# The second batch's x by rows, turned on TensorE, and a new order of the opening, in a transformer block on one core

## The chip, the core and the metric

The kernel runs on one core of one Trainium2 chip. The metric is the device time of one execution in microseconds (us); lower is better. A core has TensorE (PE in the profile, its weight loads PEld), VectorE (DVE), ScalarE (ACT), GpSimd (POOL) and SyncE (SP), which issues most of the DMAs. Each engine works through its own queue in order; they meet at semaphores.

## What is computed

Eight sequences (B = 8) of 1024 tokens of 128 numbers pass through single-head causal attention with a partial rotary embedding, a layer norm, a feed-forward layer with binarized weights and a second layer norm, all in float32:

```python
q, k, v = x @ wq, x @ wk, x @ wv                      # (8, 1024, 128) each
q, k = fractional_rope(q) / sqrt(128), fractional_rope(k) / sqrt(128)
s = q @ k.T - 1e30 * (i < j)
x = layernorm(x + softmax(s) @ v @ wo)
bw1, bw2 = mean(|w|, axis=1) * sign(w) for w1, w2     # (512, 128), (128, 512)
x = layernorm(x + gelu(x @ bw1.T + b1) @ bw2.T + b2)
```

## The kernel before

A batch c (0 to 7) is one sequence. Its 1024 tokens are 8 tiles (rows r, 0 to 7) of 128, in two halves h of 4 tiles, so that a half fills one PSUM bank of 512 columns. PSUM is held as two single banks (`next_bank`) and three pairs (`next_pair`), each handed out in turn: a task waits (`wait_freed`) until the task that had the same bank or pair three pairs or two banks earlier has been read out.

For a batch, the steps are these. x, transposed to `xT`, is split into a rounded part `xT_hi` (ScalarE, `xT_high`) and the rest `xT_lo` (GpSimd, `xT_low`; for batch 0 VectorE, `x0T_low`). `project(h, c)` makes q and k of a half with 12 matmuls of 256 columns into a pair (L631 to L633). VectorE multiplies by the tables (`rotate`, L1565 to L1568), ScalarE copies the pair to `tok` (`tok_copy`), GpSimd adds the rotated parts (`rotation_sum`, L340), TensorE turns q and k (`turn_qk(n, c)`, L641; n = 0, 1 are q and k of the first half, 2, 3 of the second), ScalarE and VectorE split them (`qkT_high`, `qkT_low`). `scores(r, c)` fills a pair; VectorE takes the maximum of the row (`row_max`, L1417), ScalarE the exponential (`exponentials`, L964). The turned probabilities come in one of two ways: in most rows VectorE transposes squares of 32 x 32 (`turn_row`, L1427) and 16 DMAs a group put the squares in place (`carry(g, c)`, L238); in rows 4 to 7 of the first and the last batch TensorE turns them (`turn_row` on TensorE, L658) and ScalarE and VectorE copy them (`row_copy`). `weigh_group` and `weigh_row` multiply with x itself (row tiles `xa[c % 2]`), `project_out` with the product of wv and wo. Then come the first norm, the feed-forward layer and the second norm.

For batch 0, x is loaded as rows into `xa[0]` and turned by TensorE (`turn_x0`). For the batches from 1 on, `xT` comes in a second load: four DMAs a batch (`stripes(c)`) bring stripes of 32 columns of x into `xq`, with pieces of 128 bytes, and VectorE transposes each half in squares (`x_squares`, L1544). The rows of x are loaded too (`tokens(c)`), since the weighing and the residual need them.

The order of each engine's queue is written out by hand, as a flat list of calls, and all lists overlap the batches: the opening below has work of batches 0, 1 and 2 side by side. The one-off preparation of the weights stands among them: `setup_wqk`, `setup_turn_wv`, `setup_wvT` and `setup_wvo` for attention, and for the feed-forward layer `setup_signs` (VectorE, four instructions on 512 columns in SBUF, L1394 to L1398), the turns `setup_turn_sgn1` and `setup_turn_sgn2` (TensorE, L532 and L540), `setup_magnitudes` and `setup_weights` (VectorE). In VectorE's queue of before the stretch from the first row_max reads: row_max(0, 0), row_max(1, 0), x_squares(0, 2), row_max(2, 0), x_squares(1, 2), turn_row(0, 0), row_max(3, 0), setup_wvo, turn_row(1, 0), (2, 0), (3, 0), qkT_low(3, 0), rotate(0, 1), rotate(1, 1), row_max(4, 0), setup_signs, row_max(5, 0), (6, 0), (7, 0), setup_magnitudes.

## Time and profile before

| | us |
|---|---|
| median of three runs | 292.16 (291.0 to 292.31) |
| the profiled execution, its own time | 291.92 |
| its span in the trace | 290.1 |
| TensorE busy | 264.5 (91%) |
| VectorE busy | 230.4 (79%) |
| ScalarE busy | 228.1 (79%) |
| GpSimd busy | 166.0 (57%) |

The profile page gives busy shares and a picture of the span in 40 slices of 7.25 us. Tables by stretch give the busy time of each engine between two points of time, with the clock that TensorE was granted. The timeline lists instructions with start and duration, and in brackets how long the engine had been idle before them and what ended that. In the trace, a matmul's span contains a tail that the next one overlaps, so the rate of matmuls is read from their starts.

### The profile page before, as it was taken

The numbers are of one execution on the slowest core, as the hardware profiler recorded it, in microseconds if no ns is written. First come the engines' busy times: TensorE is split into PE (matmuls) and PEld (weight loads), VectorE is DVE, ScalarE is ACT, GpSimd is POOL, SyncE is SP. The second block draws the span as 40 slices with busy tenths as digits, with TensorE's granted clock in tenths as the row PEclk, the third lists the DMA queues.
The fourth block names the chain that finished last, engine by engine and source line by source line (L and its number), as shares of the span: only waits on it lengthen the run. The fifth ranks groups of instructions, "written<-read, shape, count | busy, mean of one in ns | idle before, by whom it ended". The sixth has DMA issues, their size and how long they took to land.

```text
span 290.1 us, 5162 instructions
## 1 busy us (share of the span) xinstructions
PE 264.5 (91%) x1519; PEld 211.9 (73%) x1519; DVE 230.4 (79%) x581; ACT 228.1 (79%) x390; POOL 166.0 (57%) x254
## 2 busy tenths in 40 slices
PE   2778799999999999999999999999999998999660
PEld 2767689898677868786888678867876777897430
DVE  1669979999987998789879997799799359254983
ACT  3255648465679787897899999679999989998992
POOL 3151143503434297476794888759829987899123
PEclk9979889999999999999999999999999999999995
DMA  8957305147638844582577336913693320202204
GB/s 200 198 72 103 82 9 76 44 100 172 177 82 214 177 73 88 125 188 69 110 170 169 86 84 163 245 39 76 162 234 89 85 72 2 73 2 72 72 1 145
DMA packets 58010, 31.92 MB, mean 110 GB/s; under 512 B 33408, under 2 KB 54400, under 8 KB 57984
## 3 DMA queue, kind: packets, MB, share of 16 engines
q1 hardware_dynamic: 57168, 30.82, 47.3%
q10 hardware_dynamic: 816, 0.79, 0.8%
q8 instruction: 12, 0.20, 0.3%
q14 instruction: 14, 0.11, 0.1%
HBM read 9.18 MB, written 4.19 MB: 46 GB/s over the span
## 4 chain that ended last, share of the span: by engine, by line
PE 80%; DVE 5%; ACT 5%; issue 4%; POOL 2%; DMA 2%; SPq 0%; ACTq 0%; POOLq 0%; DVEq 0%
PE bank L574 17%; PE pair L555 16%; PE bank L600 5%; PE bank L641 5%; PE bank L649 5%; PE bank L650 5%; PE bank L588 4%; PE pair L618 4%; PE pair L619 4%; PE pair L631 3%; ACT res L1039 3%; PE pair L633 2%; PE pair L632 2%; PE bank L607 2%; PE pair L658 2%
## 5 line engine op out<-in xcount | busy, mean ns | idle before, releaser
L375 POOL TENSOR_TENSOR hid_lo<-hid,hid_hi 128x1024 fp32r<-128x1024 f32 x28 | 66.5, 2391 | 27.8 <-ACT hid_hi L1012 27.8
L964 ACT ACTIVATE prob<-pair,negmax 128x128 f32<-128x128 f32 (+3 forms) x64 | 47.4, 743 | 18.8 <-DVE negmax L1417 15.6
L1417 DVE TENSOR_REDUCE negmax<-pair 128x1 f32<-128x128 f32 (+3 forms) x64 | 46.8, 745 | 10.7 <-PE pair L558 10.5
L574 PE MATMUL bank<-probT,xa 128*128 128x512 f32 (+3 forms) x160 | 54.6, 484 | 0.0
L574 PEld LDWEIGHTS bank<-probT,xa 128*128 128x128 f32 x160 | 28.9, 191 | 19.7 <-issue 15.3
L555 PE MATMUL pair<-qkT_hi 128*128 128x512 f32 (+3 forms) x96 | 39.3, 409 | 1.2 <-ACT tok L979 1.2
L1427 DVE STREAM_TRANSPOSE turned<-prob 128x128 f32<-128x128 f32 (+7 forms) x56 | 39.6, 722 | 0.6 <-ACT prob L964 0.6
L340 POOL TENSOR_TENSOR tok<-rot_cos,rot_sin 128x512 f32<-128x512 f32 x16 | 20.5, 1283 | 31.9 <-ACT tok L979 31.9
L555 PE MATMUL pair<-qkT_hi,qkT_lo 128*128 128x512 f32 (+3 forms) x96 | 33.1, 345 | 0.0
L555 PE MATMUL pair<-qkT_lo,qkT_hi 128*128 128x512 f32 (+3 forms) x96 | 33.1, 345 | 0.0
L1005 ACT ACTIVATE hid<-pair,b_sb,alpha 128x1024 f32<-128x1024 f32 x28 | 32.9, 1208 | 0.1
L1012 ACT ACTIVATE hid_hi<-hid 128x1024 fp32r<-128x1024 f32 x28 | 28.6, 1054 | 0.9 <-PE bank L650 0.8
L1039 ACT ACTIVATE res<-res,ln 128x128 f32<-128x128 f32 x60 | 26.0, 492 | 3.4 <-POOL ln L369 3.4
L1573 DVE TENSOR_TENSOR qkT_lo<-bank,qkT_hi 128x512 fp32r<-128x512 f32 x32 | 21.4, 682 | 8.1 <-ACT qkT_hi L993 7.8
L334 POOL TENSOR_TENSOR xT_lo<-xT,xT_hi 128x512 fp32r<-128x512 f32 x14 | 17.9, 1286 | 16.5 <-ACT xT_hi L972 16.5
L328 POOL TENSOR_TENSOR ln<-ln,minus_half 128x4 f32<-128x4 f32 (+1 forms) x21 | 26.2, 1247 | 1.6
L993 ACT ACTIVATE qkT_hi<-bank 128x512 fp32r<-128x512 f32 x32 | 18.6, 597 | 8.8 <-PE bank L641 8.3
L979 ACT ACTIVATE tok<-pair 128x1024 f32<-128x1024 f32 x16 | 16.3, 1027 | 10.3 <-DVE rot_sin L1568 9.9
L1445 DVE SCALAR_TENSOR_TENSOR res<-bank,rinv,xa 128x128 f32<-128x128 f32 x64 | 18.9, 341 | 6.9 <-issue 3.9
L618 PE MATMUL pair<-x1T_hi,sgn1T 128*128 128x512 f32 x56 | 23.5, 420 | 0.0
L649 PE MATMUL bank<-hid_hi,sgn2T 128*128 128x512 f32 x56 | 22.9, 409 | 0.0
L631 PE MATMUL pair<-w_hi,xT_hi 128*128 128x256 f32 x64 | 20.6, 322 | 1.7 <-DVE xT_lo L1548 1.7
(114 smaller groups left out, 660.7 us busy)
## 6 DMA issues: line engine op xcount, KB each, us to landing
probT<-turned SPq DMA_DIRECT2D x96, 116.0 KB, 2.3
probT<-turned SPq DMA_DIRECT2D x128, 52.0 KB, 1.9
xq<-in_L_attn_x_dram SPq DMA_DIRECT2D x28, 128.0 KB, 3.7
xa<-in_L_attn_x_dram SPq DMA_DIRECT2D x7, 512.0 KB, 4.4
out_dram<-res SPq DMA_DIRECT2D x7, 512.0 KB, 3.2
hid<-in_L_ffn_w_dram SPq DMA_DIRECT2D x2, 256.0 KB, 3.0
out_dram<-res SPq DMA_DIRECT2D x2, 256.0 KB, 2.3
xa<-in_L_attn_x_dram ACTq DMA_DIRECT2D x1, 256.0 KB, 4.0
```

Of the source, the lines that this page charges most:

```text
L375: pool.tensor_tensor(hid_lo[:, j, :], hid[:, j, :], hid_hi[:, j, :].bitcast(F32), ALU.subtract).then_inc(s_hid_lo[j], 1)
L555: ins = pe.matmul(dst[:, lo:hi], qp[:, 0, me], kp[:, 1, lo - first:hi - first], start=n == 0, stop=n == 2 and not diagonal)
L574: ins = pe.matmul(bank_of["px", g, c][:, 0:n * P], xa[c % 2][:, j, :], probT[g][:, :, TG * j:TG * j + n, :].rearrange("p n m i -> p m n i" ...
L618: pe.matmul(dst[:, half(h)], sgn1T[:, j, :], x1T_hi[:, half(h)], start=True, stop=False)
L631: pe.matmul(dst[:, cols], xT_hi[:, me], w_hi[:, :], start=True, stop=False)
L649: pe.matmul(dst[:, :], sgn2T[:, j, :], hid_hi[:, j, half(h)], start=j == 0, stop=False)
L964: act.activation(prob[r % 3][:, 0:(r + 1) * P], pair_of["score", r, c][:, slice(*columns(r))], ACT.Exp, bias=negmax[:, r:r + 1], accum_out ...
L1005: act.activation(hid[:, j, :], pair_of["up", j, c][:, :], ACT.Gelu, bias=b1_sb[:, j:j + 1], scale=alpha1[:, j:j + 1]).then_inc(s_gelu[j], 1)
L1012: act.activation(hid_hi[:, j, :], hid[:, j, :], ACT.Copy).then_inc(s_hid_hi[j], 1)
L1039: ins = act.activation(res2[c % 2][:, t, :], res2[c % 2][:, t, :], ACT.Identity, bias=ln2[:, 6, t:t + 1], scale=ln2[:, 7, t:t + 1])
L1417: dve.tensor_reduce(negmax[:, r:r + 1], pair_of["score", r, c][:, slice(*columns(r))], axis=AX.X, op=ALU.max, negate=True).then_inc(s_max[ ...
L1427: dve.transpose(turned[g][:, :, squares(r, 0, r), :].rearrange("p k m j -> p m k j"), prob[r % 3][:, 0:(r + 1) * P].rearrange("p (m k j) - ...
```

## The change

The rows of batch 1 (`xa[1]`) are loaded once, right behind wq and wk; the stripes of batch 1 are no longer loaded, and VectorE's two `x_squares` of batch 1 go. TensorE turns the rows in eight transposes (`turn_x(h, 1)`) into the two single banks, and ScalarE copies them to `xT` (`xT_copy`). A semaphore `s_xT_pe` says that TensorE has turned a half; `s_xT`, which now counts from batch 1, says that `xT` is written. SyncE issues the stripes of batch 2 without a wait, and carry(0, 0) ahead of stripes(3). The queues of all engines are reordered through batches 0 and 1 and a little of 2: on TensorE turn_x(h, 1) stands between the two projections of batch 0, turn_qk(2, 0) behind scores(3, 0), and the four turned rows 4 to 7 one behind the other; on ScalarE tok_copy(1, 0) stands behind qkT_high(1, 0); on GpSimd rotation_sum(1, 0) stands behind the two xT_low of batch 1, and rotation_sum(1, 1) ahead of the two xT_low of batch 2. On VectorE the order behind row_copy(7, 0) changes too, in calls whose number stays the same. The diff, without that last part and the rest of the reordered lists:

```diff
--- before.py
+++ after.py
@@ -143,6 +143,7 @@
             return [sem(f"{name}{i}") for i in range(n)]
 
 
+        s_xT_pe = sems("s_xT_pe", NG)
         s_qk, s_qkT, s_score, s_px, s_attn = (
             sems("s_qk", NG), sems("s_qkT", 4), sems("s_score", NT), sems("s_px", NT), sems("s_attn", NG))
         s_x1T, s_up, s_down, s_yTok = sems("s_x1T", NG), sems("s_up", NF), sems("s_down", NG), sems("s_yTok", NG)
@@ -206,8 +207,7 @@
             sp.dma_start(xa[0][:, 0:TG, :], tokens_of(0)[:, 0:TG, :]).then_inc(s_x0_in[0], 16)
             sp.dma_start(w_raw[:, 0:D], wq[0]).then_inc(s_wqk_in, 16)
             sp.dma_start(w_raw[:, D:2 * D], wk[0]).then_inc(s_wqk_in, 16)
-            for n in range(NB):
-                sp.dma_start(*stripe(1, n)).then_inc(s_xq_in, 16)
+            sp.dma_start(xa[1][:, :, :], tokens_of(1)).then_inc(s_xa_in[1], 16)
             sp.dma_start(wv_sb, wv[0]).then_inc(s_wvo_in, 16)
             sp.dma_start(wo_sb, wo).then_inc(s_wvo_in, 16)
             sp.dma_start(w1_sb, w1.rearrange("(p f) d -> p f d", f=NF)).then_inc(s_ffn_in, 16)
@@ -217,7 +217,8 @@
 
             def stripes(c):
                 for h in range(NG):
-                    sp.wait_ge(s_xT[h], c)
+                    if c > 2:
+                        sp.wait_ge(s_xT[h], c - 1)
                 for n in range(NB):
                     sp.dma_start(*stripe(c, n)).then_inc(s_xq_in, 16)
 
@@ -249,10 +250,9 @@
                 sp.dma_start(out[c].rearrange("(n p) d -> p n d", p=P)[:, ts, :], res2[c % 2][:, ts, :]
                              ).then_inc(s_stored[c % 2], 16)
 
-            tokens(1)
             stripes(2)
+            carry(0, 0)
             stripes(3)
-            carry(0, 0)
             stripes(B - 4)
             carry(0, 1)
             carry(1, 1)
@@ -376,17 +376,17 @@
                                    ALU.subtract).then_inc(s_hid_lo[j], 1)
 
             rotation_sum(0, 0)
-            rotation_sum(1, 0)
             xT_low(0, 1)
             xT_low(1, 1)
+            rotation_sum(1, 0)
             rotation_sum(0, 1)
+            rotation_sum(1, 1)
             xT_low(0, 2)
             xT_low(1, 2)
-            rotation_sum(1, 1)
             rotation_sum(0, 2)
-            rotation_sum(1, 2)
             xT_low(0, 3)
             xT_low(1, 3)
+            rotation_sum(1, 2)
             first_factors(0, 0)
...
@@ -467,8 +467,10 @@
 
                 if task == "score":
                     pe.wait_ge(s_exp[i], c + 1)
-                if task == "x0T":
+                if task == "xT" and c == 0:
                     pe.wait_ge(s_xT_lo[i], 1)
+                if task == "xT" and c == 1:
+                    pe.wait_ge(s_xT[i], 1)
                 if task == "wvo":
                     pe.wait_ge(s_prep, 2)
                 if task == "qk":
@@ -509,13 +511,16 @@
                     wait_freed(*list(bank_of)[-1 - len(banks)])
                 return bank_of[task]
 
-            def turn_x0(h):
-
-                pe.wait_ge(s_x0_in[h], 16)
-                dst = next_bank("x0T", h, 0)
+            def turn_x(h, c):
+
+                if c == 0:
+                    pe.wait_ge(s_x0_in[h], 16)
+                else:
+                    pe.wait_ge(s_xa_in[1], 16)
+                dst = next_bank("xT", h, c)
                 for t in range(TG):
-                    ins = pe.transpose(dst[:, t * P:(t + 1) * P], xa[0][:, TG * h + t, :], ident[:, :])
-                ins.then_inc(s_xT[h], 1)
+                    ins = pe.transpose(dst[:, t * P:(t + 1) * P], xa[c][:, TG * h + t, :], ident[:, :])
+                ins.then_inc(s_xT_pe[h], 1)
 
             def setup_turn_wv():
                 pe.wait_ge(s_wvo_in, 32)
@@ -687,19 +692,21 @@
                 ins.then_inc(s_yTok[h], 1)
 
 
-            turn_x0(0)
-            turn_x0(1)
+            turn_x(0, 0)
+            turn_x(1, 0)
             project(0, 0)
+            turn_x(0, 1)
+            turn_x(1, 1)
             project(1, 0)
             turn_qk(0, 0)
             turn_qk(1, 0)
-            turn_qk(2, 0)
             setup_turn_wv()
             scores(0, 0)
+            setup_wvo()
             scores(1, 0)
             scores(2, 0)
             scores(3, 0)
-            setup_wvo()
+            turn_qk(2, 0)
             turn_qk(3, 0)
             project(0, 1)
             project(1, 1)
@@ -707,28 +714,28 @@
             scores(5, 0)
             scores(6, 0)
             scores(7, 0)
+            setup_turn_sgn1()
             turn_row(4, 0)
-            setup_turn_sgn1()
             setup_turn_sgn2()
-            project(0, 2)
             turn_row(5, 0)
+            turn_row(6, 0)
+            turn_row(7, 0)
             turn_qk(0, 1)
             turn_qk(1, 1)
+            project(0, 2)
+            turn_qk(2, 1)
+            turn_qk(3, 1)
+            scores(0, 1)
             project(1, 2)
             weigh_group(0, 0, 3, 0)
-            turn_qk(2, 1)
-            scores(0, 1)
-            turn_qk(3, 1)
...
                                bias=negmax[:, r:r + 1], accum_out=rowsum[:, r:r + 1]).then_inc(s_exp[r], 1)
 
             def xT_high(h, c):
-                act.wait_ge(s_xT[h], c + 1)
-                if c > 0:
+                if c == 0:
+                    act.wait_ge(s_xT_pe[h], 1)
+                else:
+                    act.wait_ge(s_xT[h], c)
                     act.wait_ge(s_qk[h], c)
-                src = bank_of["x0T", h, 0][:, :] if c == 0 else xT[:, half(h)]
+                src = bank_of["xT", h, 0][:, :] if c == 0 else xT[:, half(h)]
                 act.activation(xT_hi[:, half(h)], src, ACT.Copy).then_inc(s_xT_hi[h], 1)
+
+            def xT_copy(h, c):
+
+                act.wait_ge(s_xT_pe[h], c + 1)
+                act.activation(xT[:, half(h)], bank_of["xT", h, c][:, :], ACT.Copy).then_inc(s_xT[h], 1)
 
             def tok_copy(h, c):
 
@@ -1055,49 +1069,51 @@
 
             xT_high(0, 0)
             xT_high(1, 0)
+            xT_copy(0, 1)
             tok_copy(0, 0)
+            xT_copy(1, 1)
             xT_high(0, 1)
-            tok_copy(1, 0)
+            xT_high(1, 1)
             qkT_high(0, 0)
             qkT_high(1, 0)
-            xT_high(1, 1)
-            qkT_high(2, 0)
+            tok_copy(1, 0)
             exponentials(0, 0)
             exponentials(1, 0)
             exponentials(2, 0)
+            qkT_high(2, 0)
+            qkT_high(3, 0)
             exponentials(3, 0)
-            qkT_high(3, 0)
             tok_copy(0, 1)
             tok_copy(1, 1)
             xT_high(0, 2)
             exponentials(4, 0)
+            xT_high(1, 2)
             exponentials(5, 0)
             exponentials(6, 0)
             exponentials(7, 0)
             row_copy(4, 0)
-            xT_high(1, 2)
+            row_copy(5, 0)
+            row_copy(6, 0)
+            row_copy(7, 0)
             qkT_high(0, 1)
-            row_copy(5, 0)
             qkT_high(1, 1)
-            tok_copy(0, 2)
-            pxT_copy(0, 0)
             qkT_high(2, 1)
-            tok_copy(1, 2)
             qkT_high(3, 1)
             exponentials(0, 1)
...
@@ -1538,14 +1554,13 @@
 
             def x_squares(h, c):
                 if h == 0:
-                    dve.wait_ge(s_xq_in, 16 * NB * c)
-                if c > 1:
-                    dve.wait_ge(s_xT_lo[h], c)
+                    dve.wait_ge(s_xq_in, 16 * NB * (c - 1))
+                dve.wait_ge(s_xT_lo[h], c)
                 dve.transpose(xT[:, half(h)], xq[:, half(h)]).then_inc(s_xT[h], 1)
 
             def x0T_low(h):
                 dve.wait_ge(s_xT_hi[h], 1)
-                dve.tensor_tensor(xT_lo[:, half(h)], bank_of["x0T", h, 0][:, :], xT_hi[:, half(h)].bitcast(F32),
+                dve.tensor_tensor(xT_lo[:, half(h)], bank_of["xT", h, 0][:, :], xT_hi[:, half(h)].bitcast(F32),
                                   ALU.subtract).then_inc(s_xT_lo[h], 1)
 
             def rotate(h, c):
@@ -1578,25 +1593,23 @@
             x0T_low(0)
             x0T_low(1)
             rotate(0, 0)
-            x_squares(0, 1)
-            x_squares(1, 1)
             rotate(1, 0)
             qkT_low(0, 0)
             qkT_low(1, 0)
             setup_wvT()
+            x_squares(0, 2)
+            row_max(0, 0)
+            x_squares(1, 2)
+            row_max(1, 0)
+            setup_wvo()
+            row_max(2, 0)
+            turn_row(0, 0)
+            turn_row(1, 0)
+            row_max(3, 0)
+            turn_row(2, 0)
             qkT_low(2, 0)
-            row_max(0, 0)
-            row_max(1, 0)
-            x_squares(0, 2)
-            row_max(2, 0)
-            x_squares(1, 2)
-            turn_row(0, 0)
-            row_max(3, 0)
-            setup_wvo()
-            turn_row(1, 0)
-            turn_row(2, 0)
+            qkT_low(3, 0)
             turn_row(3, 0)
-            qkT_low(3, 0)
             rotate(0, 1)
             rotate(1, 1)
             row_max(4, 0)
@@ -1605,74 +1618,74 @@
             row_max(6, 0)
             row_max(7, 0)
             setup_magnitudes()
+            row_copy(4, 0)
+            setup_weights()
+            row_copy(5, 0)
+            row_copy(6, 0)
             reciprocals(0, 0)
-            setup_weights()
-            row_copy(4, 0)
-            rotate(0, 2)
+            row_copy(7, 0)
             qkT_low(0, 1)
             qkT_low(1, 1)
-            row_copy(5, 0)
+            rotate(0, 2)
+            qkT_low(2, 1)
+            qkT_low(3, 1)
+            row_max(0, 1)
             rotate(1, 2)
...
```

## Rows read from the trace of the kernel before

**Rows 1.** The page: busy us and share of each engine; TensorE in 40 slices.
```profile
PE 264.5 (91%) x1519; PEld 211.9 (73%) x1519; DVE 230.4 (79%) x581; ACT 228.1 (79%) x390; POOL 166.0 (57%) x254
...
PE   2778799999999999999999999999999998999660
```

**Rows 2.** Table by stretches: us; busy of PE, PEld, DVE, ACT, POOL; granted clock, DMA share, GB/s.
```profile
40.00:50.00 10.00, 10.00 (x75) 8.56 (x74) 8.96 (x22) 7.65 (x16) 3.51 (x3) 1.00 0.41 55
...
60.00:80.00 20.00, 20.00 (x128) 16.15 (x128) 19.99 (x48) 11.64 (x25) 6.17 (x11) 1.00 0.64 154
```

**Rows 3.** The same table in stretches of 2 us, in the opening.
```profile
14.00:16.00 2.00, 1.05 (x8) 0.87 (x8) 0.96 (x3) 1.06 (x3) 0.90 (x1) 1.00 0.74 124
...
18.00:20.00 2.00, 2.00 (x12) 1.91 (x11) 1.14 (x3) 0.60 (x1) 1.82 (x2) 0.50 0.01 1
...
36.00:38.00 2.00, 2.00 (x11) 2.00 (x11) 1.81 (x7) 1.28 (x4) 0.65 (x1) 0.50 0.21 52
```

**Rows 4.** Timeline of TensorE: start us, us, engine, line, operation, tiles, count [idle before].
```profile
8.08 0.58 PE L631 MATMUL pair<-w_hi,xT_hi 128*128 128x256 f32 x1 [1.72 <-DVE xT_lo L1548]
...
10.60 0.41 PE L633 MATMUL pair<-w_hi,xT_lo 128*128 128x256 f32 x1
...
14.95 1.10 PE L641 MATMUL bank<-ident,tok 128*128 128x128 f32 x8 [1.38 <-POOL tok L340]
...
27.88 0.47 PE L555 MATMUL pair<-qkT_hi 128*128 128x512 f32 x1 [1.18 <-ACT tok L979]
...
34.07 0.84 PE L658 MATMUL pair<-ident,prob 128*128 128x128 f32 x5 [1.88 <-ACT prob L964]
34.71 1.06 PE L532 MATMUL bank<-ident,hid 128*128 128x128 f32 x4
```

**Rows 5.** Timeline of VectorE, 12 to 38 us.
```profile
12.40 1.29 DVE L1544 STREAM_TRANSPOSE xT<-xq 128x512 f32<-128x512 f32 x2
...
19.76 0.28 DVE L1417 TENSOR_REDUCE negmax<-pair 128x1 f32<-128x128 f32 x1
...
25.34 0.68 DVE L1565 TENSOR_TENSOR rot_cos<-pair,cos_sb 128x512 f32<-128x512 f32 x1
...
26.60 0.68 DVE L1565 TENSOR_TENSOR rot_cos<-pair,cos_sb 128x512 f32<-128x512 f32 x1
...
28.60 0.79 DVE L1394 TENSOR_SCALAR hid<-hid 128x512 f32<-128x512 f32 x1
29.31 0.42 DVE L1395 TENSOR_SCALAR hid<-hid 128x512 f32<-128x512 f32 x1
29.76 1.67 DVE L1397 SCALAR_TENSOR_TENSOR hid<-hid 128x512 f32<-128x512 f32 x1
31.36 0.68 DVE L1398 SCALAR_TENSOR_TENSOR hid<-hid 128x512 f32<-128x512 f32 x1
31.96 3.08 DVE L1417 TENSOR_REDUCE negmax<-pair 128x1 f32<-128x768 f32 x3
...
36.93 0.68 DVE L1413 CAST sgn2T<-bank 128x512 fp32r<-128x512 f32 x1
```

**Rows 6.** Timeline of GpSimd around setup_signs.
```profile
27.82 1.29 POOL L340 TENSOR_TENSOR tok<-rot_cos,rot_sin 128x512 f32<-128x512 f32 x1 [8.00 <-ACT tok L979]
29.60 1.29 POOL L334 TENSOR_TENSOR xT_lo<-xT,xT_hi 128x512 fp32r<-128x512 f32 x1 [0.49 <-ACT xT_hi L972]
```

**Rows 7.** Timeline of ScalarE: exponentials(5, 0).
```profile
32.94 0.90 ACT L964 ACTIVATE prob<-pair,negmax 128x768 f32<-128x768 f32 x1 [2.64 <-DVE negmax L1417]
```

**Rows 8.** The page's groups: forms, count | busy us, mean ns of one | idle before, releaser.
```profile
L993 ACT ACTIVATE qkT_hi<-bank 128x512 fp32r<-128x512 f32 x32 | 18.6, 597 | 8.8 <-PE bank L641 8.3
```

**Rows 9.** Timeline of SyncE's queue: DMA issues.
```profile
2.23 4.83 SPq L210 DMA_DIRECT2D xq<-in_L_attn_x_dram  x4
...
24.92 11.03 SPq L238 DMA_DIRECT2D probT<-turned  x16
```

**Rows 10.** The page's DMA issues: KB each, median us from issue to landing.
```profile
xa<-in_L_attn_x_dram SPq DMA_DIRECT2D x7, 512.0 KB, 4.4
```

82 lines of the change are left out of this document (38 added, 44 removed).

## The prediction

> **What bounds the kernel now.** I began with the page's busy shares and slices: TensorE is busy 91% of the span, and its digits are 9 from the sixth slice to near the end [rows 1]. The table by stretches says the same: 10.00 of 10 us at 40 to 50, 20.00 of 20 at 60 to 80, while VectorE has 8.96 of 10 in the first and 19.99 of 20 in the second [rows 2]. A queue without a gap ends when its work ends, so the change can only act on what TensorE loses before about 40 us, and VectorE, which is as full as TensorE until 80, must be able to follow.
>
> TensorE's own lines give the losses: 1.38 us before the first turn_qk, 1.18 before scores(5, 0), 1.88 before turn_row(4, 0) [rows 4]. To that comes the clock: the granted clock is 1.00 at 14 to 16, 0.50 (1.2 GHz) at 18 to 20 and again at 36 to 38, after the gap of 1.88 us [rows 3]. At the lower level four transposes take 1.06 us by their own span, where eight take 1.10 at the upper one [rows 4], so a stretch of 3.4 us at the lower level costs about 1.7.
>
> Next, who ends those waits. turn_row(4, 0) needs exponentials(5, 0) (32.94, 0.90) [rows 7], which needs row_max(5, 0), which VectorE starts at 31.96 because setup_signs (L1394 to L1398) stands ahead of it [rows 5]. So VectorE's queue sets the opening: row_max(0, 0) at 19.76, rotate(0, 1) at 25.34, setup_signs 28.60 to 31.96, and TensorE goes on at 34.07 [rows 4, 5]. I call the start of rotate(0, 1) r and the end of setup_signs S. Before: r = 25.34, S = r + 6.62 = 31.96, TensorE's restart S + 2.11.
>
> The length of setup_signs is the odd thing. L1394 and L1395 are one operation on equal shapes and take 0.79 and 0.42; L1397 and L1398 take 1.67 and 0.68 [rows 5]. Each long one lies over a GpSimd instruction that reads SBUF: rotation_sum(0, 1) 27.82 to 29.11, xT_low(0, 2) 29.60 to 30.89, and each ends 0.3 to 0.5 us after it [rows 5, 6]. I read it as VectorE standing still until GpSimd is done, 0.37 + 0.99 = 1.36 us of the 3.36. The Trainium skill ("SBUF — State Buffer", section "Who interferes with whom") says that a VectorE instruction with two SBUF inputs, or in a two-port mode, and a GpSimd instruction that reads SBUF block each other fully, the later one waiting; these rows agree.
>
> **The change, part by part.**
>
> Loads. Four stripe issues (4.83 us of SP's queue, from 2.23) become one of xa[1] [rows 9]. A 512 KB load of x takes 4.4 us to land in the page's median [rows 10]; turn_x(0, 1) wants it at 10.8, so 8 us after its issue: hidden. The stripes of batch 2 are now issued without a wait and are wanted near 18: hidden. carry(0, 0) is 11.03 us of issues from 24.92 [rows 9] and starts when turn_row(3, 0) is done, as now; stripes(3) goes behind it (issued near 38 instead of 24) and x_squares(0, 3) wants it beyond 42: hidden, with a margin of 1 to 4 us. Nothing ahead of 8.08, where project(0, 0) starts, changes. Cost 0; bounds -0.3 to +0.3.
>
> TensorE. Eight transposes are added between project(0, 0) and project(1, 0). Four take 0.85 us apart from their tail at the lower level (1.06 less the overlap) [rows 4]; so 1.7 us of new work. project(0, 0) issues from 8.08 to 10.81 (12 matmuls, the last at 10.60) [rows 4]; the transposes then end at 12.5 and project(1, 0) at 15.3, or at 14.8 if the clock rises near 14 as before. Now 13.6. Of the 1.7 us, the 1.38 of waiting before turn_qk (14.95) swallows most: turn_qk(0, 0) starts at 14.95 to 15.1. That project(1, 0) is later by 1.2 to 1.7 costs nothing by itself, since what hangs on it (rotate(1, 0), turn_qk(2, 0)) is moved behind scores(3, 0).
>
> VectorE. The two transposes of x (1.29 us at 12.40 [rows 5]) go, but from where VectorE would now wait for project(1, 0) anyway: worth nothing there. rotate(1, 0), 1.26 long (25.34 to 26.60 [rows 5]), now ends at 16.1 to 16.5, and qkT_low(0, 0) and (1, 0) follow, ending at 17.5 to 18.2.
>
> ScalarE. Two copies of a bank are added, 0.6 each as the other bank copies (597 ns [rows 8]). xT_copy(0, 1) ends at 12.5, just when tok_copy(0, 0) could start; the second lies in idle time. tok_copy(1, 0) no longer stands ahead of qkT_high(0, 0) and (1, 0): this brings qkT_high forward by 0.3 if the clock is up.
>
> From there to r I add up the queue. scores(0, 0) starts at 17.5 (clock stays up), 17.5 (clock falls at 17.5) or 18.2 (it never rose). VectorE needs from row_max(0, 0) to r the same list as before, 5.58 us (19.76 to 25.34 [rows 5]), less one transpose (0.65), plus one qkT_low (0.6). row_max(0, 0) comes at 18.2, 18.5 or 19.3. Where matmuls run at the lower level, scores(3, 0) ends at 21.6 or 22.1, and behind it stand two turn_qk (0.9), one copy after the other (0.3 + 0.6), exponentials(3, 0) 0.8 and turn_row(3, 0) 0.6 (both narrower than the 768 columns of exponentials(5, 0), 0.90 [rows 7]). This gives r = 23.9, 24.7 or 25.3, a gain of 1.4, 0.6 or 0. I take 24.5.
>
> The Trainium skill ("TensorE: Matmul & The Clock Gate", section "Part 4: PE-mode transpose") says that transposes don't count as activity for the clock. By it the eight new ones would keep the clock down until about 21, r = 25.3. Against it stands the stretch before 38: transposes until 36.3, then a projection, and the clock came up at 38 [rows 3, 4].
>
> From r to S. The work between r and the start of setup_signs is unchanged: 3.26 us [rows 5]. Its four instructions take 0.3 + 0.4 + 0.65 + 0.65 = 2.0 alone. New is the order on GpSimd: rotation_sum(0, 1), rotation_sum(1, 1), xT_low(0, 2), xT_low(1, 2), so that four instructions of 1.29 us [rows 6] are ready one behind the other just over setup_signs, where there were two with a gap. L1394 waits for the first as now (to r + 3.75). Then it depends on who gets in when both wait. VectorE keeps going through its four: S = r + 5.75. GpSimd gets in once: S = r + 7.0. They take turns: three waits of 1.29 more, S = r + 9.5. I take r + 7.0, the middle: S = 31.5, 0.5 earlier than now.
>
> From S on. sgn1's transposes (0.44 us at the upper level) now stand ahead of turn_row(4, 0) and fall into its wait. turn_row(5) to (7) come one behind the other; turn_row(7, 0) has to wait for row_copy(4, 0), which ScalarE reaches after exponentials(7, 0), and the following turn_qk for setup_weights, whose last cast starts at 36.93 now (S + 5.0, ending S + 5.7 [rows 5]); together I estimate 0.7 us, hidden if the clock is at its lower level. project(0, 2) waits behind them, but TensorE has no lack of work: nothing else is added. So TensorE arrives 0.35 earlier against S than now if the clock falls as before, 1.4 earlier if it stays up (1.5 of slow work saved). The idle time ahead of turn_row(4, 0) would be about 1.8, as now, so it is open; I take the middle, 0.9.
>
> Sum: -0.5 (S) - 0.9 = -1.4 us. From there TensorE's digits are 9 until near 240 but for one [rows 1], and its work there is unchanged, so the end shifts by as much. The profiled execution took 291.92 us, with a span of 290.1; the median of the runs is 292.16, 0.24 above. 291.92 - 1.4 = 290.5 us.
>
> **The rivals.**
> A. The forecast, -0.8 to -2.2: 289.7 to 291.1. Chance 0.38.
> B. VectorE holds the port through setup_signs and the clock stays up: S = 24.3 + 5.75 = 30.05, 1.9 earlier, and 1.4 from the clock; that VectorE is full at 60 to 80 [rows 2] takes some back. -3.3: 288.6 us. For it: VectorE's next instruction is queued when the last ends, as L1395 behind L1394. Chance 0.22.
> C. Slower. GpSimd and VectorE take turns during setup_signs: S = 24.7 + 9.5 = 34.2, 2.2 later. TensorE idles from 31.5 to 36.3, the clock falls, 0.35 is won: +1.9, 293.8 us. It decides against the kernel from the third wait on (S > 32.3). For it: both instructions that overlapped GpSimd were held up in full [rows 5, 6]. By the skill's section on who interferes with whom the later one waits, which makes turns likely when both queues are full. Chance 0.22.
> D. VectorE cannot follow: its queue has 0.01 us of slack in 60 to 80 [rows 2], so TensorE's lead is given back in waits for row_max and qkT_low there. 291.9 us, give or take 0.7. Against it: at 40 to 50 VectorE still has 1.04 us of idle time [rows 2]. Chance 0.18.
>
> **How the numbers follow.** About 0.5% (1.5 us) is what a measurement of this kernel can tell. Faster by more: B and the larger half of A, 0.44. Within: the rest of A, D and a part of C, 0.36. Slower by more: 0.20. Range: from B less 0.4 to C plus 0.2, 288.2 to 294.0, A's own range standing inside.
>
> **What would show it.** r between 23.9 and 25.3, and project(1, 0) ending near 15; L1394 to L1398 with one more long instruction (A), none but the first (B), or all four long (C); the restart of turn_row(4, 0) near 33.6; TensorE without gaps from there. The prediction is wrong if the clock behaves otherwise in the first 20 us, if xa[1] lands after 10.8, or if gaps show up on TensorE at 45 to 90.

## The result and the profile after

| | before | after |
|---|---|---|
| median of the runs | 292.2 us (291.0 to 292.31, 4 runs) | 294.64 us (293.43 to 296.1, 4 runs) |
| ratio | 1 | 1.0097, interval 1.0067 to 1.0127 |
| profiled execution, its span | 291.92, 290.1 us | 293.43, 291.6 us |
| TensorE goes on with turn_row(4, 0) at | 34.07 us | 35.19 us |

The changed kernel is slower by 2.4 us, where the forecast was 290.5 us, a gain of 1.4. An execution more than 1.5% above the fastest of its kernel counts as slow; the medians in this document are of all executions, the ratios and their intervals of the others. The page of after, against [rows 1]: busy us and share of each engine, then TensorE and its granted clock in 40 slices.

```profile
PE 265.5 (91%) x1527; PEld 213.0 (73%) x1527; DVE 231.3 (79%) x579; ACT 230.0 (79%) x392; POOL 167.0 (57%) x254
...
PE   2778599999999999999999999999999998999660
...
PEclk9999989999999999999999999999999999999795
```

TensorE has 8 instructions more and 1.0 us more of work; the digits of its slices tell nothing new. As before, the opening has to be read line by line. First VectorE's timeline in after, against [rows 5] (start us, busy us, engine, line, operation, tiles, count, idle before):

```profile
7.15 0.23 DVE L1397 TENSOR_SCALAR hid<-hid 128x128 f32<-128x128 f32 x1 [7.15 <-DMA hid<-in_L_attn_wk_dram]
...
15.48 0.69 DVE L1580 TENSOR_TENSOR rot_cos<-pair,cos_sb 128x512 f32<-128x512 f32 x1 [2.26 <-PE pair L638]
...
24.32 0.65 DVE L1580 TENSOR_TENSOR rot_cos<-pair,cos_sb 128x512 f32<-128x512 f32 x1
...
27.54 0.80 DVE L1410 TENSOR_SCALAR hid<-hid 128x512 f32<-128x512 f32 x1
28.26 1.51 DVE L1411 TENSOR_SCALAR hid<-hid 128x512 f32<-128x512 f32 x1
29.81 1.67 DVE L1413 SCALAR_TENSOR_TENSOR hid<-hid 128x512 f32<-128x512 f32 x1
31.40 1.75 DVE L1414 SCALAR_TENSOR_TENSOR hid<-hid 128x512 f32<-128x512 f32 x1
33.07 3.07 DVE L1433 TENSOR_REDUCE negmax<-pair 128x1 f32<-128x768 f32 x3
```

rotate(0, 1) starts at 24.32, 1.02 us earlier than before. Then setup_signs is 5.53 us long (27.54 to 33.07) instead of 3.36: all four instructions are long, L1411 and L1414 too, which took 0.42 and 0.68 in [rows 5] as L1395 and L1398. What lay beside them is in GpSimd's timeline, against [rows 6]:

```profile
26.77 2.72 POOL L340 TENSOR_TENSOR tok<-rot_cos,rot_sin 128x512 f32<-128x512 f32 x2 [7.00 <-ACT tok L993]
29.45 3.15 POOL L334 TENSOR_TENSOR xT_lo<-xT,xT_hi 128x512 fp32r<-128x512 f32 x2
```

Four instructions without a gap from 26.77 to 32.60, over all of setup_signs but its last 0.5 us. They suffer too: the last two take 3.15 us together, where one takes 1.29 in [rows 6]. Last, TensorE's timeline in after, against [rows 4]:

```profile
8.82 0.58 PE L636 MATMUL pair<-w_hi,xT_hi 128*128 128x256 f32 x1 [2.77 <-DVE xT_lo L1563]
...
11.55 1.91 PE L522 MATMUL bank<-ident,xa 128*128 128x128 f32 x8
...
15.71 1.09 PE L646 MATMUL bank<-ident,tok 128*128 128x128 f32 x8 [0.27 <-POOL tok L340]
...
26.83 0.47 PE L560 MATMUL pair<-qkT_hi 128*128 128x512 f32 x1 [0.93 <-ACT tok L993]
...
31.53 0.66 PE L537 MATMUL bank<-ident,hid 128*128 128x128 f32 x4 [0.39 <-DVE hid L1413]
...
35.19 1.30 PE L663 MATMUL pair<-ident,prob 128*128 128x128 f32 x5 [3.00 <-ACT prob L971]
```

project(0, 0) starts 0.74 us later than before (8.82 against 8.08). The waits before turn_qk and scores(5, 0) shrink from 1.38 and 1.18 to 0.27 and 0.93, and the one before turn_row(4, 0) grows from 1.88 to 3.00. It waited for wk, whose landing is in the DMA issues of the first 24 us in after (KB each, median us from issue to landing):

```profile
xa<-in_L_attn_x_dram SPq DMA_DIRECT2D x1, 512.0 KB, 7.2
...
hid<-in_L_attn_wk_dram SPq DMA_DIRECT2D x1, 64.0 KB, 5.4
```

wk, issued ahead of xa[1], took 5.4 us to land. The same view of the kernel before, where stripes of 128 KB follow it one by one, has 4.6 us:

```profile
hid<-in_L_attn_wk_dram SPq DMA_DIRECT2D x1, 64.0 KB, 4.6
```

These are two single executions, and the landing of wk turned out to vary by as much within one kernel (below).

From the restart on, the two profiled executions differ by 1.12 us at 35, 0.53 at 55, about 0.7 between 144 and 272, and 1.52 from 278. The jump near the end is the clock. Table by stretches, first after, then before (us; busy of PE, PEld, DVE, ACT, POOL; granted clock, DMA share, GB/s):

```profile
274.00:276.00 2.00, 2.00 (x6) 1.58 (x5) 1.77 (x7) 2.00 (x4) 0.80 (x4) 0.50 0.80 240
```

```profile
274.00:276.00 2.00, 1.83 (x8) 1.13 (x6) 1.81 (x5) 2.00 (x4) 1.36 (x7) 1.00 0.69 208
```

So the profiled difference of 1.5 us is 0.7 from the opening and 0.8 from a stretch at 1.2 GHz shortly before the end.

### The profile page after: what moved, and what is told of

Read it like the earlier page. It is cut to its first block, busy times and chain, and to the rows that moved or that the text cites. A ratio compares the mean times of both kernels' runs of the same rounds, so it can differ in the third digit from the quotient of the medians.

```text
span 291.6 us, 5174 instructions
## 1 busy us (share of the span) xinstructions
PE 265.5 (91%) x1527; PEld 213.0 (73%) x1527; DVE 231.3 (79%) x579; ACT 230.0 (79%) x392; POOL 167.0 (57%) x254
## 4 chain that ended last, share of the span: by engine, by line
PE 79%; DVE 7%; issue 7%; ACT 3%; POOL 2%; ACTq 0%; POOLq 0%; DVEq 0%
PE bank L579 17%; PE pair L560 16%; PE bank L605 5%; PE bank L654 5%; PE bank L646 5%; PE bank L655 4%; PE pair L623 4%; PE bank L593 4%; PE pair L624 4%; PE pair L663 2%; PE bank L612 2%; PE pair L636 2%; PE pair L637 2%; PE pair L638 2%; PE bank L691 1%
## 5 line engine op out<-in xcount | busy, mean ns | idle before, releaser
L971 ACT ACTIVATE prob<-pair,negmax 128x128 f32<-128x128 f32 (+3 forms) x64 | 47.4, 743 | 21.3 <-DVE negmax L1433 17.4
L560 PE MATMUL pair<-qkT_hi 128*128 128x512 f32 (+3 forms) x96 | 38.6, 402 | 1.2 <-ACT tok L993 0.9
L334 POOL TENSOR_TENSOR xT_lo<-xT,xT_hi 128x512 fp32r<-128x512 f32 x14 | 18.5, 1330 | 11.1 <-ACT xT_hi L981 11.1
L655 PE MATMUL bank<-hid_lo,sgn2T 128*128 128x512 f32 x56 | 22.1, 395 | 0.0
```

Of the source, the lines that this page charges most:

```text
L560: ins = pe.matmul(dst[:, lo:hi], qp[:, 0, me], kp[:, 1, lo - first:hi - first], start=n == 0, stop=n == 2 and not diagonal)
L655: ins = pe.matmul(dst[:, :], sgn2T[:, j, :], hid_lo[:, j, half(h)], start=False, stop=j == NF - 1)
L971: act.activation(prob[r % 3][:, 0:(r + 1) * P], pair_of["score", r, c][:, slice(*columns(r))], ACT.Exp, bias=negmax[:, r:r + 1], accum_out ...
```

## The experiments

The theory after the result: the loss has two causes, GpSimd's new order (rotation_sum(1, 1) ahead of the two xT_low of batch 2), which makes VectorE and GpSimd take turns through setup_signs, and xa[1], which delays wk. The rivals: the order of TensorE's and VectorE's queues, the added transposes, or the clock. All medians below are of 8 to 12 runs beside 23 to 31 of the kernel before on the same chip; a ratio is to these, with its interval. Differences between medians are in us; where two kernels ran on different chips, the ratios are the better comparison.

### The changed kernel again

No edit.

> The changed kernel itself, to see how much of its loss belongs to the one profiled execution. In the first profile the loss at 55 us was 0.5 us and 0.8 us more came after 270, in a stretch at the lower clock. Theory P (the loss is made in the opening by VectorE and GpSimd taking turns over setup_signs and by the later landing of wk): ratio to before 1.006 to 1.011, the four instructions of setup_signs again 0.8, 1.5, 1.7 and 1.7 us, start of the first projection again near 8.8. Theory K (the loss is the clock's: where the lower level falls differs by execution): in a new profile the lower stretches lie elsewhere, and the loss at 55 us or after 270 moves by 1 us or more, while setup_signs stays as long.

Measured: 294.67 us, 1.0080 (1.0043 to 1.0116). Its profile has another r (23.75) but the same length from there: L1410 to L1414 and TensorE's restart are

```profile
26.98 0.80 DVE L1410 TENSOR_SCALAR hid<-hid 128x512 f32<-128x512 f32 x1
27.70 1.52 DVE L1411 TENSOR_SCALAR hid<-hid 128x512 f32<-128x512 f32 x1
29.25 1.67 DVE L1413 SCALAR_TENSOR_TENSOR hid<-hid 128x512 f32<-128x512 f32 x1
30.85 1.75 DVE L1414 SCALAR_TENSOR_TENSOR hid<-hid 128x512 f32<-128x512 f32 x1
```

```profile
34.64 1.30 PE L663 MATMUL pair<-ident,prob 128*128 128x128 f32 x5 [3.00 <-ACT prob L971]
```

The turns are thus no accident of one execution. The late project(0, 0) is one: it was expected near 8.8 again, but wk is there at 6.59 instead of 7.15, with the same queue, and the projection follows:

```profile
6.59 0.23 DVE L1397 TENSOR_SCALAR hid<-hid 128x128 f32<-128x128 f32 x1 [6.59 <-DMA hid<-in_L_attn_wk_dram]
```

```profile
8.26 0.58 PE L636 MATMUL pair<-w_hi,xT_hi 128*128 128x256 f32 x1 [1.99 <-DVE xT_lo L1563]
```

This profiled execution (291.92 us) was the fastest of eleven (to 296.71): between 38 and 283 it had no stretch at 1.2 GHz. From 60 us on its matmuls stand within 0.1 us of those of the kernel before, so it shows none of the 2.4 us of the medians. One trace isn't the median here, so the verdicts below rest on the medians and the traces give the mechanism.

### setup_signs away from GpSimd's instructions

In the changed kernel, setup_signs moves behind rotate(0, 0). The waits on s_prep are renumbered with it, and nothing else is changed.

```diff
             rotate(0, 0)
+            setup_signs()
             rotate(1, 0)
...
             row_max(4, 0)
-            setup_signs()
             row_max(5, 0)
```

> The changed kernel with setup_signs moved from behind row_max(4, 0) to between rotate(0, 0) and rotate(1, 0), where VectorE waited 2.26 us for TensorE and GpSimd was idle. Nothing is left out. Theory P: its four instructions take 0.4, 0.4, 0.7 and 0.7, 2.1 us in all, inside the wait; row_max(5, 0) comes 5.5 us earlier against rotate(0, 1), TensorE's wait before turn_row(4, 0) shrinks from 3.0 us to under 1, and the kernel is 2 to 4 us faster than the changed one, that is, 1 to 2 us faster than before (ratio to before 0.993 to 0.998). Theory K, or any theory by which setup_signs is not what TensorE waited for: within 1 us of the changed kernel.

Measured: 290.59 us, 0.9941 (0.9905 to 0.9978), 4.1 us less than the changed kernel. VectorE:

```profile
13.31 0.43 DVE L1410 TENSOR_SCALAR hid<-hid 128x512 f32<-128x512 f32 x1 [0.30 <-DMA b_sb<-in_L_ffn_b_dram]
13.65 0.42 DVE L1411 TENSOR_SCALAR hid<-hid 128x512 f32<-128x512 f32 x1
14.11 0.69 DVE L1413 SCALAR_TENSOR_TENSOR hid<-hid 128x512 f32<-128x512 f32 x1
14.72 1.76 DVE L1414 SCALAR_TENSOR_TENSOR hid<-hid 128x512 f32<-128x512 f32 x1
```

and TensorE's turn_row:

```profile
35.83 1.83 PE L663 MATMUL pair<-ident,prob 128*128 128x128 f32 x15 [0.52 <-ACT prob L971]
```

Three of the four are about as short as in any trace (0.41, 0.41 and 0.69); the fourth meets rotation_sum(0, 0). turn_row(4, 0) goes on at 33.46 (35.19 in after) without a wait; the line shown is of the rows behind it. No wait of 3.00 is left, and no stretch at 1.2 GHz around 36 (the one before it was at 19.9 to 23.3). So setup_signs' place was worth 4.1 us in the changed kernel, which is 1.7 us better than before.

### xa[1] behind wk

```diff
             sp.dma_start(w_raw[:, D:2 * D], wk[0]).then_inc(s_wqk_in, 16)
+            sp.wait_ge(s_wqk_in, 32)
             sp.dma_start(xa[1][:, :, :], tokens_of(1)).then_inc(s_xa_in[1], 16)
```

> The changed kernel with one wait more on SyncE: the load of xa[1], and all loads behind it, is issued only when wq and wk have landed. Theory P: wk lands near 6.4 as in the kernel before instead of 7.15, the first projection starts at 8.1 instead of 8.8, and the kernel is 0.5 to 0.9 us faster than the changed one, if xa[1] is there by 10.8. Rival: the stripes and weights now land later than wanted (w1, w2 near 12, stripes of batch 2 near 16), xa[1] lands at 10.5 to 11.5 and TensorE waits for it: the gain at 8 us is given back, 0 in all.

Measured: 293.55 us, 1.0057 (1.0027 to 1.0086), 1.1 less than the changed kernel by the medians and 0.7 by the ratios; the two intervals overlap, so a gain isn't shown. In the trace the weight is there 1.14 us earlier than in after (7.15), 0.58 earlier than in the changed kernel again, and project(0, 0) starts as much earlier:

```profile
6.01 0.23 DVE L1398 TENSOR_SCALAR hid<-hid 128x128 f32<-128x128 f32 x1 [6.01 <-DMA hid<-in_L_attn_wk_dram]
```

```profile
7.68 0.58 PE L637 MATMUL pair<-w_hi,xT_hi 128*128 128x256 f32 x1 [1.49 <-DVE xT_lo L1564]
```

This goes through to the restart (34.06 against 35.19, again with 3.00 us of idle time before it).

How much of it belongs to the change only all traces together can tell. With this wait, wk was there at 6.00 to 6.05 (three traces). With the stripes behind it, as in the kernel before, 6.41 to 6.87 (three traces, mean 6.65); with xa[1] right behind it, 6.35 to 7.34 (seven traces, mean 6.93). So a load behind wk delays it, and the stripes do that too. That xa[1] does it more than the stripes isn't shown: the means differ by 0.28 us and the ranges overlap. What this edit takes off is for the most part a delay that the kernel before has as well.

Both edits together (the last two):

> Both edits: setup_signs between the two rotations of batch 0, and xa[1] issued when wq and wk have landed. Theory P: the two gains add up, 2.5 to 4.5 us faster than the changed kernel, 1.5 to 2.5 faster than before (ratio 0.991 to 0.996). Rival: the weights w1, w2, b1, b2 land after 13 because their issue is held too, and setup_signs, which waits for them, holds up rotate(1, 0) and qkT_low: slower than the kernel with setup_signs early alone by 0.5 to 2 us.

Measured: 294.3 us, 1.0089 (1.0059 to 1.0119): 3.7 us worse than the early setup_signs alone. The wait that helped wk holds back b1 and b2, which setup_signs needs:

```profile
13.26 1.52 DVE L1411 TENSOR_SCALAR hid<-hid 128x512 f32<-128x512 f32 x1 [1.19 <-DMA b_sb<-in_L_ffn_b_dram]
```

It waited for the load, then met GpSimd's instructions once more (13.21 to 17.31) and took turns with them, now ahead of qkT_low. The two don't add, since the edit of the loads moved the other into a collision.

### The one line on GpSimd, both ways

In the kernel before, with nothing else of the change:

```diff
             rotation_sum(0, 1)
+            rotation_sum(1, 1)
             xT_low(0, 2)
             xT_low(1, 2)
-            rotation_sum(1, 1)
```

> The kernel before with one line moved on GpSimd: rotation_sum(1, 1) ahead of xT_low(0, 2) and xT_low(1, 2), as in the changed kernel. This adds the suspected cause to the kernel before and nothing else. Theory P (turns over setup_signs): L1394 to L1398 take 0.8, 1.5, 1.7 and 0.7 instead of 0.8, 0.4, 1.7 and 0.7, so setup_signs ends 1.1 us later (33.0), and the kernel is 0.5 to 1.2 us slower than before (ratio 1.002 to 1.004). Rival (the order on GpSimd costs nothing by itself): setup_signs unchanged within 0.2 us, ratio 0.999 to 1.001.

Measured: 294.4 us, 1.0078 (1.0049 to 1.0107). This one line, by itself, costs as much as the whole change did. VectorE and TensorE:

```profile
29.56 0.80 DVE L1394 TENSOR_SCALAR hid<-hid 128x512 f32<-128x512 f32 x1
30.28 1.52 DVE L1395 TENSOR_SCALAR hid<-hid 128x512 f32<-128x512 f32 x1
31.84 1.67 DVE L1397 SCALAR_TENSOR_TENSOR hid<-hid 128x512 f32<-128x512 f32 x1
33.43 0.68 DVE L1398 SCALAR_TENSOR_TENSOR hid<-hid 128x512 f32<-128x512 f32 x1
```

```profile
36.14 0.74 PE L658 MATMUL pair<-ident,prob 128*128 128x128 f32 x5 [2.99 <-ACT prob L964]
```

Against [rows 5] only L1395 grows, from 0.42 to 1.52: one more turn, 1.1 us, and the wait before turn_row(4, 0) grows by the same (1.88 to 2.99). The median moved by 2.3. The mean granted clock of its executions is 0.970 against 0.9745 of the kernel before beside it; of a 292 us span that is (0.0299 - 0.0255) / 0.5 x 292 = 2.6 us more at 1.2 GHz, worth 1.3. That the longer gap of TensorE is what lowers the clock isn't shown, and the one trace speaks against it: behind the gap of 2.99 us the clock stays up, and its first stretch at 1.2 GHz is at 18 to 24, before the moved line runs. That stretch and a wk that landed 0.46 us later are also why the restart at 36.14 is 2.07 us behind that of before, not 1.1.

And the line taken back in the changed kernel (rotation_sum(1, 1) behind the two xT_low):

> The changed kernel with rotation_sum(1, 1) put back behind xT_low(0, 2) and xT_low(1, 2) on GpSimd. Theory P: one of the three extra waits goes, since xT_low(0, 2) is ready only half a us after rotation_sum(0, 1) ends: the second instruction of setup_signs takes 0.4 instead of 1.5, setup_signs ends 1.1 us earlier against rotate(0, 1), and the kernel is 0.7 to 1.2 us faster than the changed one (ratio to before 1.004 to 1.006). Rival (order on GpSimd does not matter): 1.008 as the changed kernel.

Measured: 292.81 us, 1.0013 (0.9979 to 1.0047), 1.9 less than the changed kernel. L1411 is 0.41 again and S comes at r + 7.69 in place of r + 8.75; the wait before turn_row(4, 0) is 2.53. It isn't the r + 6.62 of before, because GpSimd still has two instructions ready in a row: the change also moved xT_high(1, 2) forward on ScalarE, and xT_low(1, 2) waits for that. ScalarE in after, then in before:

```profile
29.14 0.63 ACT L981 ACTIVATE xT_hi<-xT 128x512 fp32r<-128x512 f32 x1
```

```profile
36.65 0.63 ACT L972 ACTIVATE xT_hi<-xT 128x512 fp32r<-128x512 f32 x1
```

So by these traces, of the 2.1 us by which setup_signs ended later against r, half is owed to the line on GpSimd and half to this one on ScalarE; no run moved the latter by itself, so its share in the median is open.

With this order and the wait of the loads together:

> The changed kernel with both suspected costs taken off and setup_signs where it was: rotation_sum(1, 1) behind the two xT_low of batch 2, and xa[1] issued when wq and wk have landed. If the two costs are all that made it slower than before (1.9 us and 1.1 us when taken off singly, against a loss of 2.4), the rest of the change is worth about 0.6 us and the kernel comes to 291.5 to 292.0, ratio 0.996 to 1.000. Rival: the two costs overlap, and something else in the change costs as well: ratio 1.002 or more.

Measured: 291.7 us, 1.0002 (0.9970 to 1.0033). The two edits together undo the loss: 1.9 and 1.1 singly, 3.0 together by the medians (by the ratios 0.7, 0.2 and 0.8%, which is 2.3 us). Against the order on GpSimd alone (1.0013) the wait of the loads adds nothing that the intervals show. What remains of the change is worth nothing that can be measured, though its opening is shorter (restart at 33.01, before 34.07). In the trace it is even 2.5 us ahead of before from 60 to 187 us. Then TensorE waits for squares of the turned probabilities, where before has no gap, which takes about 1.2 us of the lead:

```profile
189.72 3.70 PE L580 MATMUL bank<-probT,xa 128*128 128x512 f32 x8 [0.96 <-DMA probT<-turned]
```

The stretch at 1.2 GHz near the end takes another 1.1:

```profile
272.00:274.00 2.00, 2.00 (x6) 1.54 (x6) 1.40 (x6) 1.41 (x3) 0.89 (x5) 0.50 0.86 257
```

So a lead from the opening doesn't reach the end for sure, as the prediction's sum had it. The same wait stands in four other traces that are ahead of before at that point, and is missing in others that are further ahead; what decides it is open.

### Is the room for setup_signs a gift of the change?

In the kernel before, setup_signs behind rotate(1, 0):

> The kernel before with setup_signs moved from behind row_max(4, 0) to behind rotate(1, 0). Theory P (setup_signs ahead of row_max(5, 0) is what TensorE waits for in both kernels): the queue loses 3.4 us at 28.6 and gains 2 to 3 near 15, of which 1.6 lie in VectorE's wait there; qkT_low(0, 0) comes 0.5 to 1.5 later; 1.5 to 3 us faster than before, ratio 0.990 to 0.995. If so, the gain of the changed kernel with setup_signs early (ratio 0.994) is not owed to the rows of x at all. Rival (the room for setup_signs is there only because the change took away VectorE's transposes of x): same as before or slower, ratio 0.998 or more.

Measured: 291.52 us, 0.9986 (0.9964 to 1.0009). It left the crowded place, but the new one isn't free there:

```profile
15.12 0.41 DVE L1394 TENSOR_SCALAR hid<-hid 128x512 f32<-128x512 f32 x1
...
16.51 1.76 DVE L1398 SCALAR_TENSOR_TENSOR hid<-hid 128x512 f32<-128x512 f32 x1
```

```profile
19.01 1.09 PE L641 MATMUL bank<-ident,tok 128*128 128x128 f32 x4 [2.70 <-DVE qkT_lo L1573]
```

qkT_low stands behind it and TensorE waits 2.70 us for that. In the changed kernel setup_signs went between rotate(0, 0) and rotate(1, 0), into VectorE's wait for project(1, 0) (2.26 us before 15.48 in after), which the vanished transposes of x and the late project(1, 0) leave open. The two places are thus not the same, and both gains have to be taken from the kernel before: 0.6 us here, within the interval, against 1.7 there (the 4.1 contain the 2.4 that the change lost). That the room is a gift of the change fits this, but isn't shown: the place between the two rotations was not tried in the kernel before.

### The added transposes behind project(1, 0)

turn_x(0, 1) and turn_x(1, 1) stand behind project(1, 0), and ScalarE's copies follow.

```diff
             project(0, 0)
+            project(1, 0)
             turn_x(0, 1)
             turn_x(1, 1)
-            project(1, 0)
```

> The changed kernel with the eight transposes of batch 1 behind project(1, 0) instead of ahead of it, and ScalarE's copies for them moved behind tok_copy(0, 0) to match. The unprofiled executions of the changed kernel spread from 293 to 296.7, the profiled ones (291.9 and 293.4) lie low in it. Theory K2 (transposes between the two projections break up the run of matmuls by which the clock comes up, so that in part of the executions the opening stays at 1.2 GHz one stretch longer): the median falls by 1 us or more against the changed kernel, to 293.5 or less, and the spread narrows. Theory P alone: rotate(1, 0) earlier by 1.5 us, where it delays nothing; median within 0.5 us of the changed kernel's 294.7.

Measured: 293.95 us, 1.0071 (1.0039 to 1.0103), 0.7 less than the changed kernel, which the intervals don't part. rotate(1, 0) starts 2 us earlier (13.52 against 15.48), yet the restart of turn_row(4, 0) is at 34.95 with 2.99 us of wait: the place of the transposes isn't what cost there.

### Weights first

wq and wk are issued ahead of xa[0], once with the early setup_signs of the changed kernel and once in the kernel before:

```diff
-            sp.dma_start(xa[0][:, 0:TG, :], tokens_of(0)[:, 0:TG, :]).then_inc(s_x0_in[0], 16)
             sp.dma_start(w_raw[:, 0:D], wq[0]).then_inc(s_wqk_in, 16)
             sp.dma_start(w_raw[:, D:2 * D], wk[0]).then_inc(s_wqk_in, 16)
+            sp.dma_start(xa[0][:, 0:TG, :], tokens_of(0)[:, 0:TG, :]).then_inc(s_x0_in[0], 16)
```

> The changed kernel with setup_signs between the two rotations of batch 0 (290.6 us so far) and with wq and wk issued ahead of the first half of xa[0]. The landing of wk at 6.9 to 7.3 starts the chain to project(0, 0). Theory P: wk lands near 6, xa[0] near 5, project(0, 0) starts near 7.8 instead of 8.6, and the kernel gains 0.5 to 0.9 us: 289.7 to 290.1, ratio to before 0.990 to 0.993. Rival: the rows of batch 0 now come later and take wk's place in the chain, or TensorE reaches setup_turn_wv before its data: ratio 0.994 or more.

> The kernel before with wq and wk issued ahead of the first half of xa[0], nothing else. It measures what the landing of wk is worth in the kernel before. Theory P: project(0, 0) starts 0.4 to 0.8 us earlier, and the kernel is 0.3 to 0.8 us faster, ratio 0.997 to 0.999. Rival: the start is earlier but VectorE's queue takes it back: 1.000 within 0.001.

Measured: 291.93 us, 0.9999 (0.9975 to 1.0022), 1.3 worse than the early setup_signs alone; and 294.28 us, 1.0073 (1.0043 to 1.0102), 2.1 worse than before. wk is there at 4.7 and 4.5, but now the transposes of x are late. In the kernel before with weights first:

```profile
7.15 1.94 PE L517 MATMUL bank<-ident,xa 128*128 128x128 f32 x8 [7.15 <-DMA xa<-in_L_attn_x_dram]
```

and project(0, 0) starts at 9.65 instead of 8.08. The half of xa[0], issued third, took 5.4 and 5.6 us to land in the two kernels, 3.3 to 3.6 when issued first. I read it as x and the weights sharing what the DMA engines move in the first 7 us, so that a place in the queue only hands the delay on. The second run also prices a late start of project(0, 0): 1.57 us later in the trace, 2.1 in the median. In its trace, the fastest of its eight executions, only 0.8 us of that are left from 60 us on.

### The versions that were to beat both

The early setup_signs with weights first and GpSimd's old order, and without weights first:

> As the first of these four, with rotation_sum(1, 1) behind the two xT_low of batch 2 as well. With setup_signs gone from behind row_max(4, 0) no VectorE instruction there needs a second SBUF input, so theory P expects no gain from this order now: within 0.5 us of the first of these four. A gain of 1 us or more would say that the order on GpSimd costs by something else than the turns over setup_signs.

> The changed kernel with setup_signs between the two rotations of batch 0 and rotation_sum(1, 1) behind the two xT_low of batch 2; the loads as in the changed kernel. The same edit of order brought 0.9 us where wq and wk were issued first, against an expectation of nothing: in that profile the first wait for tok moved, not setup_signs. If the order has a value of its own once setup_signs is gone, this kernel comes to 289.5 to 290.0, ratio 0.990 to 0.993. If the 0.9 us was the scatter of the clock, it stays at 290.6, ratio 0.994 to 0.996.

Measured: 291.01 us, 0.9973 (0.9953 to 0.9993), 0.9 less than with the new order; and 290.43, 0.9926 (0.9897 to 0.9955), 0.2 less than with the new order. Once setup_signs is elsewhere the order on GpSimd is worth nothing that both pairs show; the 0.9 of the first pair is as large as the scatter, so it stays open. The traces show how large that scatter is: with setup_signs early, the clock falls to 1.2 GHz somewhere between 18 and 27 us in four of six and stays up there in two. From the start of project(0, 0) to r it takes 17.4 to 18.7 us where the clock fell (leaving out the version that waited for b1 and b2) and 15.9 where it didn't. With setup_signs in its old place no trace of the changed kernel had that fall (six traces, 15.5 us).

Last, in the second of these, setup_signs waits only for w1 and w2; b1 and b2 get a semaphore of their own, on which setup_weights waits:

```diff
             def setup_signs():
-                dve.wait_ge(s_ffn_in, 16 * 4)
+                dve.wait_ge(s_ffn_in, 16 * 2)
...
                 dve.wait_ge(s_prep_pe, 3)
+                dve.wait_ge(s_b_in, 32)
```

> As the one before, with b1 and b2 counted by a semaphore of their own, which setup_weights waits for, so that setup_signs waits for w1 and w2 alone. In the profile with setup_signs early its first instruction waited 0.3 us for b and its last one took 1.76 instead of 0.68, since rotation_sum(0, 0) began 0.3 us before it. Theory P (the later one waits out the whole other instruction): started 0.3 us earlier, the last one comes ahead of rotation_sum(0, 0) or nearly, takes 0.7 in part of the executions, and rotation_sum waits instead; rotate(1, 0) starts up to 1.4 us earlier; 0 to 0.7 us faster than the one before. Rival: the last instruction still comes second: same time.

Measured: 289.49 us, 0.9902 (0.9872 to 0.9931), the lowest of all, though its interval overlaps that of the version without this edit. VectorE, GpSimd and TensorE:

```profile
12.34 0.42 DVE L1410 TENSOR_SCALAR hid<-hid 128x512 f32<-128x512 f32 x1
...
13.73 1.78 DVE L1414 SCALAR_TENSOR_TENSOR hid<-hid 128x512 f32<-128x512 f32 x1
```

```profile
13.56 1.40 POOL L340 TENSOR_TENSOR tok<-rot_cos,rot_sin 128x512 f32<-128x512 f32 x1 [10.48 <-ACT tok L993]
```

```profile
33.42 1.83 PE L663 MATMUL pair<-ident,prob 128*128 128x128 f32 x15 [0.52 <-ACT prob L971]
```

setup_signs lies 1 us earlier than in the first version with it early, and the rows behind turn_row(4, 0) 2.4 us, but the edit is hardly the reason: wk was there at 6.35 here and at 6.94 and 7.29 in the two versions without it, setup_signs starts 1.28 us behind rotate(0, 0) against 1.27 in the second of them, and the clock, which fell at 18 to 25 in both, stayed up here. The last instruction still meets rotation_sum(0, 0), which had started 0.17 us before it: the collision was moved along, not removed.

## Why the prediction was wrong

- **r, taken 24.5.** Measured 24.32: near it by luck, by two errors that cancel. project(0, 0) was 0.74 late, and the rest of the opening 0.9 faster than the middle case. Of these, 0.6 is the case in which the clock stays up, which happened; 0.3 no term had. In the changed kernel again r was 23.75, just below the range of 23.9 to 25.3. The table by stretches of after, against [rows 3]:

```profile
16.00:18.00 2.00, 0.93 (x9) 0.70 (x7) 1.80 (x5) 1.77 (x4) 2.00 (x2) 1.00 0.00 0
18.00:20.00 2.00, 1.70 (x13) 1.52 (x13) 2.00 (x6) 0.86 (x3) 1.40 (x2) 1.00 0.00 0
```

  Before, 18 to 20 was at 0.50. The Trainium skill ("TensorE: Matmul & The Clock Gate", section "Part 4: PE-mode transpose") says that transposes don't count as activity for the clock, by which r would have been 25.3; the trace speaks against it here, with eight of them at 11.55 to 13.11 between two projections and no fall of the clock before 35.

- **Loads at nothing, within 0.3.** Open. "Nothing ahead of 8.08 changes" looked only at what is issued ahead of wk, not at what is behind it. project(0, 0) was 0.74 later in after, 0.18 in the changed kernel again, and over seven traces against three 0.28, with ranges that overlap (8.02 to 9.01, 8.08 to 8.54). The term had no reason for what is issued behind wk, but a cost beyond its 0.3 isn't shown. xa[1] itself took 7.2 us where 4.4 was assumed, and was still in time for 11.55.

- **project(1, 0) ends near 15.** Held: rotate(1, 0) starts at 15.48, and turn_qk, at 15.71, has waited only 0.27.

- **From r to S, taken 7.0 of 5.75, 7.0 and 9.5.** This is the step that failed: S was put at 31.5, 0.5 us earlier than before, and came at 33.07, 1.1 later. Measured 8.75 (after) and 8.77 (again), 7.72 where one more instruction of GpSimd is ready (before, new order) and 6.62 before: the engines take turns as long as both have work ready. Rival C had that mechanism, and its three more waits of 1.29 stand for four long instructions measured; each further turn costs 1.1, not 1.29, so C's 9.5 (its own terms add up to 9.6) was 0.75 too long. The prediction counted the four instructions of GpSimd rightly, but put them down to the order on GpSimd alone; the last is ready in time only because xT_high(1, 2) stands earlier on ScalarE. "C decides from S > 32.3": S was 33.07. The Trainium skill ("SBUF — State Buffer", section "Who interferes with whom") agrees: it has the later one wait. I had even written that this makes turns likely, and gave C only 0.22, because VectorE's next instruction is queued when the last ends. GpSimd's is too.

- **The restart, near 33.6 with about 1.8 us idle; 0.9 won after S.** Measured 35.19 with 3.00. From there the profile regained 0.6 by 55 us, near the 0.35 of the case in which the clock falls; but the stretch at 1.2 GHz near the end (0.8) took more than that, and no step had it, since "the end shifts by as much" took all of TensorE's work behind 40 us as fixed. The same waits of TensorE stand at the end of both kernels; of the sixteen profiled executions nine have the clock at 0.50 for some us between 270 and 278 (after among them) and seven don't (before and the changed kernel again among them). What decides it was not settled.

- **The rivals.** C's 293.8 was 0.8 short of 294.64, although its S was too late by more than 1 us: its direction and mechanism held, its size didn't, and what makes up the rest isn't shown. B (no turns, the clock up) and A (one turn) are out. D is out too: TensorE has 10.00 of 10 us at 40 to 50 and no gap at 60 to 80, where VectorE has 0.32 us left in after:

```profile
60.00:80.00 20.00, 20.00 (x132) 16.45 (x131) 19.68 (x48) 11.26 (x24) 6.43 (x12) 1.00 0.62 148
```

- **The size stays partly open.** In the profiles a turn costs 1.1 us at the restart, in the medians 1.9 to 2.3. For the kernel before with one line moved, the lower mean clock would fill the gap; for the changed kernel it doesn't: its mean is 0.976 against 0.9745, and its executions spread over 291.9 to 296.7 us. Both traces of the changed kernel are of executions below its median, and behind 60 us they stand 0.0 and 0.5 to 0.7 us behind that of before until the clock near the end. That the order on GpSimd costs about 2 us is shown by the medians in both directions; where more than 1.1 of it is lost no trace shows.
